# W_O^T loaded in blocks and turned on VectorE, and new orders for pair 0, the loop and the last pair of a fused graph layer

## The reference

```python
z_l = einsum('bnd,ed->bne', h, W_lang); z_g = einsum('bnd,ed->bne', h, W_grav); v = einsum('bnd,ed->bne', h, W_V)
zn = z_l / maximum(norm(z_l), EPS)
A_l = maximum(einsum('bnd,bmd->bnm', zn, zn), 0.0) * not_eye
sq = sum(z_g * z_g)
d2 = maximum(sq + swapaxes(sq) - 2.0 * einsum('bnd,bmd->bnm', z_g, z_g), 0.0)
A_g = exp(-d2 / (2.0 * sigma * sigma)) * not_eye
K = w_l * row_stochastic(A_l * adj) + (1.0 - w_l) * row_stochastic(A_g * adj)
out = einsum('bnd,ed->bne', einsum('bnm,bmd->bnd', K, v), W_O)
x = layernorm(x + out)
```

## Time and profile before

| | us |
|---|---|
| median of 3 runs | 656.93 (656.71 to 657.33) |
| the profiled execution, whole | 658.0 |
| its span, first to last instruction | 656.3 |
| PE busy with matmuls in the span | 641.7 |
| DVE busy | 536.7 |
| ACT busy | 381.2 |
| POOL busy | 140.8 |

### The profile page before, as it was taken

One profiled execution on the slowest core, in us unless ns is written; L12 is line 12 of the kernel. 1 busy time (PEld: TensorE's weight loads), 2 busy tenths in 40 slices (PEclk: granted clock), 3 DMA queues, 4 the chain that ended last, 5 costly groups with the idle time before them and its releaser, 6 DMA issues.

```text
span 656.3 us, 10731 instructions
## 1 busy us (share of the span) xinstructions
PE 641.7 (98%) x2860; PEld 529.5 (81%) x2860; DVE 536.7 (82%) x1432; ACT 381.2 (58%) x707; POOL 140.8 (21%) x288
## 2 busy tenths in 40 slices
PE   8999999999999999999999999999999999999895
PEld 7878778888888888888888888888888888888684
DVE  5874798888798888889798888879888887978776
ACT  5444444647475564757466564846556475745646
POOL 3441002122212112222211212221220222221023
PEclk9999999999999999999999999999999999999998
DMA  9321647285766838475674837476582848367403
GB/s 294 75 65 38 171 152 172 79 255 110 216 158 189 210 99 250 102 239 125 192 193 133 247 84 247 108 224 156 170 229 81 262 91 253 82 196 237 160 18 128
DMA packets 141509, 106.48 MB, mean 162 GB/s; under 512 B 40112, under 2 KB 115632, under 8 KB 141488
## 3 DMA queue, kind: packets, MB, share of 16 engines
q1 hardware_dynamic: 140768, 104.40, 56.4%
q0 software_dynamic: 288, 1.05, 0.5%
q10 hardware_dynamic: 432, 0.79, 0.3%
HBM read 65.80 MB, written 40.40 MB: 162 GB/s over the span
## 4 chain that ended last, share of the span: by engine, by line
PE 86%; DVE 8%; ACT 2%; DMA 1%; SPq 1%; issue 1%; POOL 0%; POOLq 0%; DVEq 0%
PE bank L1387 56%; PE bank L1459 15%; PE bank L1464 12%; PE bank L1416 2%; SPq L410 1%; DVE hT_raw L924 1%; DMA xq<-x_spill 1%; DVE p_lo L1031 1%; DVE hT_lo L932 1%; DVE m_lo L984 1%; DMA xs<-in_L_gnn_W_lang 0%; DVE work L1078 0%; DVE wvo_lo L955 0%; DVE x_nat L963 0%; DVE x_blk L1238 0%
## 5 line engine op out<-in xcount | busy, mean ns | idle before, releaser
L1031 DVE SCALAR_TENSOR_TENSOR p_lo<-bank,m_scale,p_hi 128x512 fp32r<-128x512 f32 x128 | 93.5, 743 | 27.2 <-ACT p_hi L736 27.0
L1464 PE MATMUL bank<-hT_lo,m_hi 128*128 128x512 f32 x384 | 107.9, 389 | 0.0
L736 ACT ACTIVATE p_hi<-bank,m_scale 128x512 fp32r<-128x512 f32 x128 | 84.9, 684 | 36.9 <-PE bank L1464 36.8
L1387 PE MATMUL bank<-p_hi,hT_hi 128*128 128x512 f32 x256 | 99.7, 390 | 0.6 <-DVE p_lo L1031 0.6
L1387 PE MATMUL bank<-wvo_hi,hT_hi 128*128 128x512 f32 x256 | 99.9, 390 | 0.1
L1387 PE MATMUL bank<-wvo_hi,hT_lo 128*128 128x512 f32 x256 | 99.6, 389 | 0.0
L1387 PE MATMUL bank<-p_lo,hT_hi 128*128 128x512 f32 x256 | 99.6, 389 | 0.0
L1387 PE MATMUL bank<-wvo_lo,hT_hi 128*128 128x512 f32 x256 | 99.6, 389 | 0.0
L1464 PEld LDWEIGHTS bank<-hT_lo,m_hi 128*128 128x128 f32 x384 | 72.1, 188 | 15.1
L607 POOL TENSOR_TENSOR rnorm<-norm,minus_half 128x2 f32<-128x2 f32 x32 | 35.3, 1103 | 218.2 <-DVE norm L1059 218.2
L751 ACT COPY xs<-bank 128x512 f32<-128x512 f32 x64 | 37.5, 587 | 64.8 <-PE bank L1387 64.8
(11 more groups left out here) (159 smaller groups left out, 1276.8 us busy)
## 6 DMA issues: line engine op xcount, KB each, us to landing
x_blk<-in_x SPq DMA_DIRECT2D x128, 128.0 KB, 3.3
x_spill<-xs SPq DMA_DIRECT2D x30, 512.0 KB, 3.5
xq<-x_spill SPq DMA_DIRECT2D x120, 128.0 KB, 3.0
x_nat<-in_x SPq DMA_DIRECT2D x30, 512.0 KB, 4.2
out_y<-y SPq DMA_DIRECT2D x30, 512.0 KB, 3.3
k_spill<-work SPq DMA_DIRECT2D x30, 256.0 KB, 2.2
work<-k_spill SPq DMA_DIRECT2D x120, 64.0 KB, 2.1
r_row<-r_spill SPq DMA_DIRECT2D x32, 128.0 KB, 3.4
```

The lines of the kernel that those rows point to most:

```text
L736: nc.scalar.activation(p_hi[:, :, j, g, :], src[:].rearrange("p (b n) -> p b n", b=2), ACT.Copy, scale=m_scale[:, g, j:j + 1]).then_inc(pr ...
L1031: nc.vector.scalar_tensor_tensor(out=p_lo[:, :, j, g, :], in0=src[:].rearrange("p (b n) -> p b n", b=2), scalar=m_scale[:, g, j:j + 1], in ...
L1387: last = pe.matmul(dst, lhsT, rhs, start=(n == 0), stop=(n == len(steps) - 1))
L1464: last = pe.matmul(pbank(k)[:], md_hi[:, g, 0] if i == 0 else m_hi[:, g, i, c], lo[i], start=False, stop=(i == DT - 1))
```

## The change

W_O is no longer transposed on PE. It comes in 16 DMAs in place of two, block by block, so that only the 32x32 blocks are left to be turned, and DVE turns them in four instructions (`wo_turn`), one for each 128x512 slab. ACT makes the high part from that copy (`wo_hi`), DVE the low part (`wo_lo`), both from SBUF. The four WO_TURN units are gone, 18 units stay. The first unit takes its matmuls in another order, so that those which need only high parts go first, and there are six warming matmuls in place of eight. POOL takes the masks of the diagonal blocks in another order. The lists of pair 0, of the loop and of the last pair are in a new order on SP, ACT and DVE, and on PE in the last pair. In pair 0 `turn(1, 0)` and the small scalar steps stand behind the fourth projection's low part. At the end the scale is done from mean and reciprocal deviation directly.

```diff
-        prep_units = [(UPPER, L, i) for i in range(DT)] + [(UPPER, G, 0)]
         for i in range(1, DT):
-            prep_units += [(MIRROR, L, i), (WO_TURN, None, i - 1)]
-            if i == DT - 1:
-                prep_units += [(WO_TURN, None, i)]
-            prep_units += [(UPPER, G, i)]
+            prep_units += [(MIRROR, L, i), (UPPER, G, i)]
-        WARM = 8
+        WARM = 6
...
-            for b in range(2):
-                sp.dma_start(y[:, b], w_o.rearrange("(b k p) d -> b p k d", b=2, p=P)[b]).then_inc(y_moved[b], 16)
+            for j in range(P // BLK):
+                for k in range(DT):
+                    cols = w_o.rearrange("(m c) d -> c m d", c=BLK)[:, :, k * P + j * BLK:k * P + (j + 1) * BLK]
+                    sp.dma_start(raw[3][j * BLK:(j + 1) * BLK, k].rearrange("c (m a) -> c m a", a=BLK),
+                                 cols).then_inc(wo_loaded, 16)
...
                 load_blocks(p + 1, 1)
+                return_x(q, 1)
                 load_blocks(p + 2, 0)
-                return_x(q, 1)
                 spread_r(q, 1)
                 spill_k(q, 0)
+                load_x(q, 0)
                 return_k(q, 0)
-                load_x(q, 0)
                 spill_k(q, 1)
                 store(q - 1, 0)
                 load_x(q, 1)
                 spill_x(p, 0)
+                store_r(p, 0)
                 return_k(q, 1)
-                store_r(p, 0)
+                spread_r(p, 0)
                 return_x(p, 0)
                 store(q - 1, 1)
+                store_r(p, 1)
                 spill_x(p, 1)
-                store_r(p, 1)
-                spread_r(p, 0)
...
+            def wo_turn(i):
+
+                dve.wait_ge(wo_loaded, 16 * DT * (P // BLK))
+                dve.wait_ge(w_lo_ready, DT)
+                nc.vector.transpose(wo_plain[:, i], raw[3][:, i]).then_inc(wo_turned, 1)
...
+                if (kind, g, i) == (UPPER, L, DT - 1):
+                    wo_turn(0)
+                    wo_turn(1)
+                if (kind, g, i) == (UPPER, G, 0):
+                    wo_lo(0)
+                    wo_lo(1)
+                    wo_turn(2)
+                    wo_turn(3)
+                if (kind, g, i) == (UPPER, G, 1):
+                    wo_lo(2)
+                    wo_lo(3)
...
+                proj_lo_part(p, 0)
+                gram(q, 0, L)
                 gauss_masked(q, 0)
-                gram(q, 0, L)
-                proj_lo_part(p, 0)
                 cosine_masked(q, 0)
+                proj_lo_part(p, 1)
                 row_factors(q, 0)
-                proj_lo_part(p, 1)
-                turn_x(q, 1)
                 proj_lo_part(p, 2)
                 proj_lo_part(p, 3)
+                if type(p) is int and p == 0:
+                    turn(1, 0)
+                    shares()
+                    dve.wait_ge(scal_steps, 8)
+                turn_x(q, 1)
+                kernel_sum(q, 0)
+                inverse_masked(q, 1)
+                proj_lo_part(p, 4)
                 gram(q, 1, G)
-                proj_lo_part(p, 4)
-                kernel_sum(q, 0)
...
+            def first_block(dst):
+
+                hi, lo = w_parts[L]
+                for r in range(DT + 1):
+                    if r < DT:
+                        pe.wait_ge(w_hi_ready, r + 1)
+                        pe.matmul(dst[:], hi[:, r, 0:P], hi[:, r], start=(r == 0), stop=False)
+                    if r > 0:
+                        pe.wait_ge(w_lo_ready, r)
+                        pe.matmul(dst[:], hi[:, r - 1, 0:P], lo[:, r - 1], start=False, stop=False)
+                        last = pe.matmul(dst[:], lo[:, r - 1, 0:P], hi[:, r - 1], start=False, stop=(r == DT))
```

More of the change, by code:

```diff
@@ L664, in _ @@
                 mean(q, b)
[L665 removed]
                 layer_norm(q, b)
[L667 to L669 removed]
+            for b, t in ((0, 1), (0, 0), (1, 0), (1, 1)):
+                last_spread(b, t)
         @block.scalar
@@ L901, in _ @@
             squares(q, 1)
+            last_kt_hi_part(1)
             proj_hi_part(p, 11)
-            last_kt_hi_part(1)
-            normalise(q, 0)
             normalise(q, 1)
-            for b in range(2):
-                for t in range(NT):
-                    last_squares(b, t)
-            for b in range(2):
-                last_normalise(b, 0)
+            last_squares(0, 0)
+            last_squares(0, 1)
+            last_squares(1, 0)
+            last_squares(1, 1)
+            last_normalise(0, 0)
+            last_normalise(1, 0)
             act.wait_ge(last_normed[1][0], 1)
@@ L1007, in _ @@
                     turn(0, 1)
-                if (kind, i) == (WVO, 1):
+                    for k in (1, DT - 1):
+                        diagonals(G, k)
                     scales(G)
@@ L1170, in residual @@
                     dve.wait_ge(x_loaded[b], 16 * (q + 1))
-                    dve.wait_ge(y_moved[b], 16 * (q + 1))
+                    if type(q) is int and q == 0:
+                        dve.wait_ge(wo_turned, DT)
+                    else:
+                        dve.wait_ge(y_moved[b], 16 * q)
                 nc.vector.scalar_tensor_tensor(
@@ L1193, in pair @@
                 proj_lo_part(p, 7)
-                inverse_masked(q, 1)
                 gauss_masked(q, 1)
@@ L1214, in pair @@
                 kt_lo_part(q, 1)
-                proj_lo_part(p, 9)
+                inverse_masked(p, 0)
                 turn_x(p, 0)
@@ L1218, in pair @@
                 residual(q, 1, 0)
-                inverse_masked(p, 0)
                 residual(q, 1, 1)
@@ L1408, in prepare @@
                     emptied(u - 4)
-                if kind == UPPER:
+                if (kind, g, i) == (UPPER, L, 0):
+                    last = first_block(dst)
+                elif kind == UPPER:
                     cols = slice(i * P, D)
@@ L1421, in prepare @@
                         last = pe.transpose(dst[:, r * P:(r + 1) * P], m_hi[:, g, r, rows].bitcast(F32), ident[:])
-                elif kind == WO_TURN:
-                    for b in range(2):
-                        pe.wait_ge(y_moved[b], 16)
-                    for r in range(DT):
-                        last = pe.transpose(dst[:, r * P:(r + 1) * P], raw[3][:, r, rows], ident[:])
                 else:
@@ L1575, in _ @@
             q = p - 1
-            for k in range(2 * DT):
-                project(p, 1, k)
+            project(p, 1, 0)
+            project(p, 1, 1)
+            project(p, 1, 2)
+            project(p, 1, 3)
+            project(p, 1, 4)
+            project(p, 1, 5)
+            project(p, 1, 6)
+            project(p, 1, 7)
             value(p, 1, 0, 0)
-            for b in range(2):
-                for t in range(NT):
-                    x_tile(p, 1, b, t)
+            x_tile(p, 1, 0, 0)
+            x_tile(p, 1, 0, 1)
+            x_tile(p, 1, 1, 0)
+            x_tile(p, 1, 1, 1)
             last_gram_turn(p, 0, L)
+            k_times_v(q, 0, 0)
+            k_times_v(q, 0, 1)
             last_gram_turn(p, 0, G)
-            for t in range(NT):
-                k_times_v(q, 0, t)
+            last_gram_turn(p, 1, G)
             last_gram_turn(p, 1, L)
             value(p, 1, 0, 1)
-            last_gram_turn(p, 1, G)
-            for t in range(NT):
-                k_times_v(q, 1, t)
             pe.wait_ge(last_gram[0][L], 1)
             value(p, 1, 1, 0)
+            k_times_v(q, 1, 0)
             last_k_turn(p, 0)
+            k_times_v(q, 1, 1)
             pe.wait_ge(last_gram[0][G], 1)
@@ L1596, in _ @@
             last_k_turn(p, 1)
-            for b in range(2):
-                for t in range(NT):
-                    last_k_times_v(p, b, t)
+            last_k_times_v(p, 0, 0)
+            last_k_times_v(p, 0, 1)
+            last_k_times_v(p, 1, 0)
+            last_k_times_v(p, 1, 1)
 _INS = ['x', 'adj', 'L0_gnn_W_lang', 'L0_gnn_W_grav', 'L0_gnn_W_V', 'L0_gnn_W_O', 'L0_gnn_gate_logit',
```

236 lines of the change are left out of this document (127 added, 109 removed).

## The result

The changed kernel takes 660.02 us (median of 7, 658.87 to 662.75) against 657.11 us (656.71 to 657.72) for the one before: ratio 1.0046, 95% interval 1.0033 to 1.0059. It is slower by more than the 0.2% that can be told. The forecast was 652.9 us, faster. The third rival happened, W_O late and the clock falls, and with it came a loss in the last pair that no rival had.

What follows compares the result with a forecast made beforehand. PE was taken to bound the loop (513.00 of 513 us busy). Gains of 2.1 (weight preparation), 1.3 (pair 1) and 0.6 us (last pair and tail), 4.0 off 656.93, gave 652.9 us; range 650.2 to 657.0.

Steps and rivals of the forecast that it cites:

- third rival: Weight preparation: W_O lands late (from T = 19.5), PE runs dry, its clock falls; slower, 659.1 us at T = 21; chance 0.10.
- The landing of W_O: Weight preparation: 8,192 packets of 128 bytes load in 6.5 us; W_O lands at 17.8, gain 2.1 us.
- T: Time at which W_O has landed, in the weight preparation; bounds 14.8 to 19.2 us, taken as 17.8.
- The walk from T: Weight preparation: DVE's new list of turns and low parts lets the first WVO start at about T + 7.0.
- third rival's formula: Weight preparation, slowdown for late W_O: at T = 21, 21 - 19.9 + 3 - 1.9 = 2.2 us.
- about 3 us on the fall: Weight preparation: units at half speed after PE's gap cost about 3 us more, in the case of chance 0.10.
- T + 25.2: Weight preparation: forecast start of projection 4 of pair 0, by PE's own sum; 45.1 before.
- Pair 1 and the loop: Pair 1: all its time without a matmul goes, 1.3 us won; loop: cost 0, low parts stay ahead of PE.
- The last pair: Last pair and tail: a new 1.3 us stall replaces most old ones; 0.6 us won together, bounds -0.2 and 2.3.
- pushes this to about 599.3: Last pair, SP's queue: `spill_x` behind two stores of r delays the issue of `r_row` from 598.41 to about 599.3.

Runs made afterwards that it cites:

- e7_split: Changed kernel with W_O's 128-byte pieces in four DMAs, three on SP's queue and the fourth on ACT's: 658.11 us.
- e11_split_last: Changed kernel with a quarter of W_O's pieces on ACT's queue and the last pair's old lists: 655.80 us.
- e12_wv_behind: Changed kernel with W_O in 512-byte pieces by four DMAs and W_V issued only once W_O landed (folded weights wrong): 665.41 us, one execution.
- e8_best: Changed kernel with W_O's old path (transposed on PE) and the last pair's old lists, keeping the new start and loop: 653.87 us.
- e1_old_wo: Changed kernel with the old way of W_O put back (two plain loads, four transposing units on PE), all new lists kept: 656.02 us.
- e2_last_old: Changed kernel with the last pair's old lists on SP, ACT, DVE and PE, W_O's new path kept: 659.39 us.

## Why the prediction was wrong

1. **The landing of W_O: the step that failed.** "I take the middle, 12.7 ns and 6.5 us, T = 17.0, and add 0.8 us": the turns began at 21.47, and at 19.02 to 22.90 in the four kernels with this very start. The price of a piece held (13.8 ns). Wrong was that the load lasts only as long as its pieces keep the engines busy. Two things were left out. SP's queue did not keep the engines supplied: from 14 to 18 us half their time went unused, and with a quarter of the pieces on ACT's queue the turns began at 17.12 and 17.23 (e7_split, e11_split_last). And W_V's megabyte on POOL's queue had 0.69 of the engines from 10 to 14 us. For the wide pieces the second was shown by e12_wv_behind, 3.3 us. For the 128-byte pieces it is argued from the shares; a run with W_V behind them was not made. Why SP's queue supplied so unevenly stays open.
2. **The walk from T.** The first WVO at T + 7.0 was at T + 8.6 (30.08 - 21.47). The turns took 1.30 as priced. The four low parts of W_O^T took 2.37 + 1.92 us, not 2.6. The last section shows beside what.
3. **The clock.** The third rival's formula gives 659.6 us for T = 21.47, and the median is 660.0. Its mechanism was right: PE ran dry for 4.63 us and the clock fell. Its price was not, and the near agreement is luck. It put about 3 us on the fall. By the trace the start lost 3.2 us beyond the late landing (49.88 against T + 25.2 = 46.67): 1.6 of them are the slower low parts of point 2, and 1.6 are the matmuls at half speed between the first WVO and projection 0 (13.23 us against 11.6). e7_split against e11_split_last says 2.4. The rest of the agreement is a last pair worse than forecast against pairs 0 to 14 better than forecast. With a chance of 0.10 the rival was far too low, because T was.
4. **Pair 1 and the loop.** Right. 1.3 us of idle time won in 62 to 86 us, nothing lost in the loop. The stretch from projection 4 to the last pair won 2.1; the other 0.8 shows as no idle time, since the same 2,442 matmuls took 552.4 us in place of 553.2, and its cause is not shown.
5. **The last pair.** 0.6 us were to be won; by e8_best against e1_old_wo 2.15 were lost. The step that failed is "pushes this to about 599.3". It counted the two stores of r ahead of `spread_r`, but not that `return_x`, ahead of it as well, waits for the spill of x to land (4.9 us), which no longer happens under those stores. `r_row` was issued 2.0 us after projection 0 and not 0.3 before. The kind of loss, a stall of DVE that stops PE before projection 4, was as forecast; it was twice as long, and the clock fell behind it.

Four kernels form a square. With the new last lists, W_O's new path costs 660.0 - 656.0 = 4.0 us (changed kernel, e1_old_wo); with the old ones 659.4 - 653.9 = 5.5 us (e2_last_old, e8_best). The last lists cost 0.6 us beside the new path and 2.15 beside the old. The two estimates of each differ by 1.5 us, and the intervals of the four kernels are 0.8 to 1.0 us to either side, so whether the parts add up is not told. What is left, the new start and loop, wins 657.1 - 653.9 = 3.2 us.

## What to carry to other kernels

Price a load in small pieces from three sides: the time that the pieces take on the engines, the rate at which one queue gives them out (which here differed threefold between executions), and what other queues move at the same time. When an instruction list is reordered, walk the queue that is moved past with all its waits, not only with its issue times: one waiting instruction ahead of a small transfer made it late by more than the stall it was to remove. Count a fall of the clock behind such a gap of PE as likely, not as a tail: it came behind 4.63 us here and behind 1.72 us in one of two executions. When a forecast comes out near the time, check its terms one by one; here a wrong price was hidden by another loss of the same size.
